# Two layers of cross-attention and routed experts on one core: from seven blocks with barriers to one block, with buffers placed by hand

## The chip, the cores and the metric

The kernel runs on one core of a Trainium2 chip. The metric is the device time of one execution in microseconds (us); lower is better. Five engines run their own instruction streams: PE (TensorE), DVE (VectorE), ACT (ScalarE), POOL (GpSimd) and SP (SyncE), which here only issues DMAs. They meet through semaphores.

## What is computed

4096 tokens (4 batches of 1024) with 256 features pass two layers in float32. Each layer adds a cross-attention over 64 context rows of its batch and then a feed-forward part with 8 experts:

```python
x = x + attention0(layernorm(x), ctx, mask)   # 8 heads of 64, masked keys
x = x + ffn0(layernorm(x))    # softmax router, best expert, capacity 640 rows, relu(x W1) W2, DFF 1024
x = x + attention1(layernorm(x), ctx)         # 16 heads of 64
x = x + ffn1(layernorm(x))    # best 2 of 8 experts, silu(x W11) * (x W12), then W2, DFF 512
```

A token over an expert's capacity in `ffn0` keeps its own row.

## The kernel before

The work is six stages, one after the other: setup of layer 0, attention of layer 0, experts of layer 0 (E0), setup of layer 1, attention of layer 1, experts of layer 1 (E1). A matrix product in float32 precision is made of three: every operand is split into a high part (`_hi`, written by ACT) and a rest (`_lo`, written by DVE or POOL), and hi·hi, hi·lo and lo·hi are summed in PSUM.

**Constants and setup** (`constants`, `attention_setup`, L130 to L359). DVE and POOL write constants in a first block (L159). Then SP loads the context, wk, wv, wqT, wo, the bias and the router, in layer 0 also x and the zero fills (L252 to L259, L189 to L199). PE makes keys and values, DVE puts them into `kd` and `vd` (L334 to L338), tiles that are cleared first (DVE L318, POOL L265). Then come the setup products: m = wqT·kd (PE L288; ACT `m_hi` L309; DVE `m_lo` L352), two psum tiles in turn in layer 1 and four in layer 0, and n = vd·wo with the bias (PE L297 to L300; ACT L314; DVE L357), over four psum banks. With m and n, attention needs only xn·m for the scores and prob·n for the output. All of m comes first, then all of n, b by b over the four batches.

**Attention** (`attention`, block at L487) runs over 32 tiles of 128 tokens in a software pipeline: iteration t goes from -8 to 36 and does, of different tiles, the gather of an expert's row (layer 1, t + 8, POOL L639), the statistics (t + 6), the normalisation `xn` (t + 5, L864), its transposes (t + 4, L527), the scores (t + 3, L546), maximum and exp (t + 2, ACT L604), the division (t + 1, POOL L636), the transposes of prob (t, L518), the output product (t, L561), the router (t - 3) and the scatter of rows to the experts (POOL L626). So the first useful exp comes at t = -2. Layer 1 ends with `plan` on DVE (L736 to L774), which makes the table `tab` of 39 tiles of 256 rows, with first row and expert of each. SP then writes 8 zero tails behind the experts' rows (L503 to L506).

**Experts.** `experts_capacity` (E0, block at L933) handles 8 experts of 640 rows: SP loads rows (L920), weights (L912, L916) and stores y (L956). Beside it, ACT and POOL split E1's raw weights (L1053, L1125), which SP loads and stores (L924, L929, L931). `experts_top2` (E1, block at L1189) loops over the 39 tiles: SP loads `E_up_w` (L1204), `w2` (L1212) and rows `xin` (L1219); PE transposes (L1239), multiplies up (L1266) and down (L1251); POOL adds the weighted rows into the output (L1386).

**What sets the order around the change.** Each stage is one or two blocks. At the end of a block every engine drains and meets a barrier. Between attention and experts `phase` (L120 to L128) also clears all semaphores and runs one more barrier. Buffers are opened and closed in stacks, so that the next stage's tiles may lie where the last one's were:

```python
def phase(self):
    self.nc.clear_and_free_semaphores(self.sems)
    self.sems = []
    self.nc.all_engine_barrier()
```

## Time and profile before

| | |
|---|---|
| median of 3 runs | 1207.63 us (1204.55 to 1209.05) |
| the profiled execution | 1209.9 us |
| its span in the profile | 1208.2 us |
| busy: PE / DVE / ACT / POOL | 1062.8 / 758.5 / 667.7 / 518.8 us |
| mean granted PE clock | 0.947 of full speed |
| moved by DMA | 159.36 MB, 181 GB/s over the span with both sides counted |
| chain that ended last | PE 21%, DMA 5%, DVE 2% of the span |

The span runs from the first to the last instruction; the execution's own time has 1.7 us around it. Timeline rows give start and duration in us, engine and line, operation with what it writes and reads, and in brackets how long the engine had been idle and what ended that. The stages lie in the span as follows: setup 0 until 37, attention 0 until 216, E0 from 220 to 468, setup 1 until 532, attention 1 with the plan until 820, E1 from 830 to the end.

### The profile page before, as it was taken

The page shows a single profiled execution, that of the slowest core. Times are in us where ns is not written, and L with a number is a line of the kernel's source. Part 1 is how long each engine was busy: PE and PEld are TensorE (multiplying, and loading weights), DVE is VectorE, ACT ScalarE, POOL GpSimd, SP SyncE. Part 2 cuts the span into 40 slices and gives each one's busy share as a digit, 9 for nine tenths or more (in the row PEclk, how much of TensorE's full clock was granted, in tenths as well). Part 3 has the DMA queues.
Part 4 walks back from the last instruction along what each step waited for, and adds up shares of the span by engine and source line. Part 5 has one row for each costly group of instructions (what it writes and reads, how often), then busy time and mean ns, then how long its engine had stood idle before and what let it go on. Part 6 is the DMA issues. An engine that isn't in the chain of part 4 may idle for free. (4 is left out here: it accounts for less than half of the span.)

```text
span 1208.2 us, 26203 instructions
## 1 busy us (share of the span) xinstructions
PE 1062.8 (88%) x7956; PEld 1000.7 (83%) x7956; DVE 758.5 (63%) x2287; ACT 667.7 (55%) x2466; POOL 518.8 (43%) x527
## 2 busy tenths in 40 slices
PE   6799995599999996868999999822999999999995
PEld 5588884599999995847999999822899999999995
DVE  6678876344444442675677777570776766766764
ACT  2588884344444440248999999711444444444442
POOL 1346776333333331035568887660233333333333
PEclk9899998699999997989999999965999999999998
DMA  8700001476666736001112221135557657388632
GB/s 298 310 2 23 28 32 47 167 249 219 218 218 217 235 110 182 4 23 31 36 47 75 76 72 63 54 133 211 150 141 218 164 144 232 57 280 253 162 62 35
DMA packets 86487, 159.36 MB, mean 132 GB/s; under 512 B 7682, under 2 KB 65924, under 8 KB 84356
## 3 DMA queue, kind: packets, MB, share of 16 engines
q1 hardware_dynamic: 69028, 131.20, 31.3%
q0 software_dynamic: 17376, 27.15, 10.9%
q8 instruction: 40, 0.66, 0.2%
q14 instruction: 43, 0.35, 0.1%
HBM read 157.37 MB, written 61.25 MB: 181 GB/s over the span
## 5 line engine op out<-in xcount | busy, mean ns | idle before, releaser
L1386 POOL DMA_INDIRECT out<-E_y,E_dest x78 | 121.1, 1553 | 262.1 <-DVE E_y L1347 241.8
L1266 PE MATMUL psum<-E_xT_hi,E_up_w 128*128 128x256 f32 x1248 | 225.1, 280 | 7.1 <-DMA E_up_w<-up 5.7
L604 ACT ACTIVATE L_prob<-psum,L_neg_max 128x64 f32<-128x64 f32 x768 | 228.6, 362 | 2.6 <-DVE L_neg_max L828 2.5
L1266 PEld LDWEIGHTS psum<-E_xT_hi,E_up_w 128*128 128x128 f32 x1248 | 194.1, 190 | 7.7 <-issue 6.0
L604 ACT ACTIVATION_READ_ACCUMULATOR L_prob<-psum,L_neg_max 128x1 f32 x768 | 195.3, 256 | 0.0
L1266 PE MATMUL psum<-E_xT_lo,E_up_w 128*128 128x256 f32 x624 | 174.3, 279 | 0.0
L1300 ACT ACTIVATE E_sg<-psum 128x256 f32<-128x256 f32 x156 | 60.0, 384 | 176.9 <-PE psum L1266 175.2
L1355 DVE TENSOR_TENSOR E_hf<-psum,E_sg 128x256 f32<-128x256 f32 x156 | 65.9, 422 | 94.8 <-ACT E_sg L1300 93.7
L561 PE MATMUL psum<-L_n_hi,L_pT_hi 128*128 128x256 f32 x384 | 109.6, 285 | 10.9 <-DVE L_pT_lo L835 10.9
L1266 PEld LDWEIGHTS psum<-E_xT_lo,E_up_w 128*128 128x128 f32 x624 | 118.4, 190 | 0.0
L636 POOL TENSOR_TENSOR L_prob<-L_prob,L_rcp 128x512 f32<-128x512 f32 (+1 forms) x64 | 94.3, 1474 | 37.4 <-DVE L_rcp L794 36.4
L561 PE MATMUL psum<-L_n_lo,L_pT_hi 128*128 128x256 f32 x384 | 109.3, 285 | 0.0
L561 PE MATMUL psum<-L_n_hi,L_pT_lo 128*128 128x256 f32 x384 | 109.3, 285 | 0.0
L1044 ACT ACTIVATE E_h_hi<-psum 128x256 fp32r<-128x256 f32 (+1 forms) x128 | 55.9, 437 | 89.3 <-PE psum L987 89.3
L1088 DVE SCALAR_TENSOR_TENSOR E_h_lo<-psum,E_h_hi 128x256 fp32r<-128x256 f32 (+1 forms) x128 | 62.8, 491 | 54.8 <-ACT E_h_hi L1044 54.1
L1004 PE MATMUL psum<-E_w_hi,E_h_hi 128*128 128x256 f32 x320 | 91.1, 285 | 0.0
L1004 PE MATMUL psum<-E_w_hi,E_h_lo 128*128 128x256 f32 x320 | 90.6, 283 | 0.0
L1004 PE MATMUL psum<-E_w_lo,E_h_hi 128*128 128x256 f32 x320 | 90.5, 283 | 0.0
L1251 PE MATMUL psum<-E_w_hi,E_h_hi 128*128 128x256 f32 x312 | 90.1, 289 | 0.0
L1251 PE MATMUL psum<-E_w_hi,E_h_lo 128*128 128x256 f32 x312 | 86.9, 279 | 0.0
L1251 PE MATMUL psum<-E_w_lo,E_h_hi 128*128 128x256 f32 x312 | 86.9, 279 | 0.0
L546 PE MATMUL psum<-L_m_hi,L_xT_hi 128*128 128x512 f32 x192 | 83.8, 437 | 3.4 <-ACT L_prob L604 3.4
(202 smaller groups left out, 3121.1 us busy)
## 6 DMA issues: line engine op xcount, KB each, us to landing
E_up_w<-up SPq DMA_DIRECT2D x39, 2048.0 KB
E_w<-in_w SPq DMA_DIRECT2D x39, 512.0 KB
w<-in_w SPq DMA_DIRECT2D x16, 1024.0 KB, 15.7
E_xin<-rows SPq DMA_DIRECT2D x39, 260.0 KB, 2.8
E_raw<-in_w SPq DMA_DIRECT2D x16, 512.0 KB, 6.9
up<-E_raw_hi SPq DMA_DIRECT2D x16, 512.0 KB, 5.9
up<-E_raw_lo SPq DMA_DIRECT2D x16, 512.0 KB, 3.7
rows<-zero SPq DMA_DIRECT2D x8, 640.0 KB
```

The costliest lines, as they stand in the source:

```text
L546: mm = e.matmul(bank, a[:, (t + 3) % 2, c, :], m[:, b, c, q * 512:(q + 1) * 512], start=(layer == 1 and c == 0 and j == 0), stop=(c == KC ...
L561: mm = e.matmul(o, a[:, r, :], m[:, b, r, :], start=(r == 0 and j == 0), stop=(r == PR - 1 and j == 2))
L604: last = e.activation(prob[:, q, h * KEYS:(h + 1) * KEYS], scores_ps(t)[:, h * KEYS:(h + 1) * KEYS], ACT.Exp, bias=nmx[:, q, h, :], accum_ ...
L636: e.tensor_tensor(pr, pr, rc[:, q, :, :].to_broadcast([P, H, KEYS]), ALU.mult).then_inc(s_p, 1)
L1004: mm = q.matmul(bank, a[:, h, m, c * P:(c + 1) * P], w[:, par, m, :], start=(k == 0), stop=(k == 3 * FC - 1))
L1044: q.activation(h_hi[:, h, m, 0:cn * P], ps[:, UP_BANK + m % 4, 0:cn * P], ACT.Relu).then_inc(s_hhi, 1)
L1088: q.scalar_tensor_tensor(h_lo[:, h, m, 0:cn * P], ps[:, UP_BANK + m % 4, 0:cn * P], 0.0, h_hi[:, h, m, 0:cn * P].bitcast(F32), ALU.max, AL ...
L1251: mm = q.matmul(ps[:, Y_BANK + c, 0:D], a[:, par, m, c * P:(c + 1) * P], w[:, par, m, :], start=(k == 0), stop=(k == 3 * FC - 1))
L1266: mm = q.matmul(bank, up_w[:, par, half, w, c, m * P:(m + 1) * P], x[:, c, :], start=(k == 0), stop=(k == 3 * KC - 1))
L1300: q.activation(sg[:, m, :], ps[:, UP_BANK + m, 0:T1], ACT.Silu).then_inc(s_sg, 1)
L1355: q.tensor_tensor(hf[:, m, :], ps[:, UP_BANK + m, T1:2 * T1], sg[:, m, :], ALU.mult).then_inc(s_hf, 1)
L1386: q.indirect_dma_start(p.out[:, :], bass.IndirectOffsetOnAxis(ap=dest[:, par, c, :], axis=0), y[:, par, c, :], None, compute_op=ALU.add).t ...
```

## The change

All stages now stand in one block, so each engine goes through all its stages without a barrier; counted waits on semaphores take the place of barriers. `phase`, the stacks and the clearing are gone. Semaphores with the same meaning serve both layers, and layer 1 waits for counts above those of layer 0 (`counted(base)`). Buffers have fixed places in one arena of 172 KiB (`p.at(kib, ...)`). Beyond that:

- The constants' block is gone; SP's first loads stand at the program's start. `kd` is cleared on POOL, ahead of `vd`. x is waited for by quarters.
- m of batch b is made in iteration t = b - 8 of the attention loop and n of batch b in t = b - 4, on PE, ACT and DVE. n has three psum banks (4 to 6) where it had four.
- SP loads w1 and w2 of expert 0 when n is done, E1's first raw weights when the last attention output is made, and expert 0's rows when the scatters have landed.
- The loads of setup 1 (ctxT, wk, wv, wqT) are issued inside E0's last expert. On ACT the last raw split stands inside that expert's hidden(7,1).
- The first four gathers of layer 1 have their own buffer. The 8 zero tails are issued by ACT, after its part of attention 1.
- For E1, SP waits for the table and the last scores, issues up(0) and w2(0), and only then waits for the scatters and issues xin(0).

The core of the diff:

```diff
-    def phase(self):
-        self.nc.clear_and_free_semaphores(self.sems)
...
-        self.nc.all_engine_barrier()
...
+    def at(self, kib, name, shape, dt=F32):
...
+        return self.nc.alloc_sbuf_tensor_at(name, shape, dt, offset=self.arena + int(kib * 1024))
...
+    N_BANK, RING_N = 4, 3
...
+    def loads(e):
...
+        else:
+            e.wait_ge(before.s_w1lo, E)
+            e.wait_ge(before.s_w2lo, E)
+            e.wait_ge(before.s_up, before.UPS * (E - 1))
+        e.dma_start(ctxT[:, :, :], ins["ctxT"].rearrange("(c p) k -> p c k", p=CP)).then_inc(s_w, 16)
...
+    def gpsimd(e):
+        if layer == 1:
+            e.wait_ge(before.s_rlo, 2 * E)
+            e.wait_ge(before.s_sthi, 16 * 2 * E)
+            e.wait_ge(before.s_stlo, 16 * 2 * E)
+        e.memset(kd[:, :, :, :], 0.0).then_inc(s_zero, 1)
+        if layer == 1:
+            e.wait_ge(before.s_up, before.UPS * E)
+        e.memset(vd[:, :, :, :], 0.0).then_inc(s_zero, 1)
...
+    def tensor_n(e, b):
...
+        for r in range(PR):
+            need(e, s_nlo, b * PR + r - RING_N + 1)
...
     def tensor(e):
+        e.wait_ge(p.s_sel, 3)
         for t in iters:
+            if ok(t + 8) and t < -4:
+                setup.tensor_m(e, t + 8)
+            if -4 <= t < 0:
+                setup.tensor_n(e, t + 4)
+            if t == -3:
+                setup.need(e, setup.s_mlo, setup.MS)
...
+            if t == 0:
+                setup.need(e, setup.s_nlo, setup.NS)
...
     def sync(q, late):
+        setup.need(q, setup.s_nlo, setup.NS)
+        load_w1(q, 0)
+        load_w2(q, 0)
+        rows_from.need(q, rows_from.s_out, NT)
+        for j in range(2):
+            load_raw(q, 0, j)
+        rows_from.rows_landed(q)
         load_x(q, 0)
-        for j in range(2):
-            load_raw(q, 0, j)
         load_w1(q, 1)
         load_w2(q, 1)
         for e in range(E):
             if e + 1 < E:
                 load_x(q, e + 1)
+            else:
+                late(q)
             store_raw(q, e, 0)
...
+                if m == 3 and (h == 0 or last):
+                    split_raw(e, h)
...
+        q.wait_ge(rows_from.s_tab, 2)
+        rows_from.need(q, rows_from.s_sim, NT)
+        load_up(0, 0)
+        load_w2(0, 0)
+        rows_from.rows_landed(q)
         load_x(0, 0)
-        load_up(0, 0)
-        load_w2(0, 0)
...
+        @block.scalar
+        def _(e):
+            att0.scalar(e)
+            exp0.scalar(e)
+            att1.scalar(e)
+            att1.tails(e)
+            exp1.scalar(e)
```

How the instructions move on SP at the end of E0. The kernel before, from the last expert's raw stores to the last load of setup 1; a branch is the end or the start of a block, where SP meets the other engines:

```order
L929 DMA up<-E_raw_hi 128x1024
L931 DMA up<-E_raw_lo 128x1024
L956 DMA rows<-E_y 128x3x256
L956 DMA rows<-E_y 128x2x256
L933 UNCONDITIONAL_BRANCH
L249 UNCONDITIONAL_BRANCH
L253 DMA L_ctxT<-in_ctxT 96x2x256
L254 DMA L_wk<-in_wk 96x2x1024
L255 DMA L_wv<-in_wv 96x2x1024
L256 DMA L_wqT<-in_wqT 128x8x256
L257 DMA L_wo<-in_wo 128x8x256
```

The changed kernel, the same stretch (the loads of the next setup are L266 to L269):

```order
L266 DMA L_ctxT<-in_ctxT 96x2x256
L267 DMA L_wk<-in_wk 96x2x1024
L268 DMA L_wv<-in_wv 96x2x1024
L269 DMA L_wqT<-in_wqT 128x8x256
L1021 DMA up<-E_raw_hi 128x1024
L1023 DMA up<-E_raw_lo 128x1024
L1021 DMA up<-E_raw_hi 128x1024
L1023 DMA up<-E_raw_lo 128x1024
L1053 DMA rows<-E_y 128x3x256
L1053 DMA rows<-E_y 128x2x256
L279 DMA L_wo<-in_wo 128x8x256
```

The four large loads of setup 1 have moved from behind two block ends to ahead of the last expert's raw stores; wo stays behind the last y store. No branch is left between the stages.

On ACT at the start of layer 1, before: the last two rows of n's loop, the blocks' seam and the first rows of attention:

```order
L314 ISA
L314 ACTIVATE L_n_hi<-psum 128x256
L310 REGISTER_ALU
L310 COMPARE_AND_BRANCH
L248 UNCONDITIONAL_BRANCH
L582 UNCONDITIONAL_BRANCH
L591 ACTIVATE L_xT_hi<-psum 128x256 x3
L604 ACTIVATE L_prob,L_sum<-psum,L_neg_max 128x64 x16
L591 ACTIVATE L_xT_hi<-psum 128x256
L604 ACTIVATE L_prob,L_sum<-psum,L_neg_max 128x64 x16
```

The changed kernel, from m to exp of tile 1 (L340 is n_hi, L657 xT_hi, L670 exp):

```order
L335 ACTIVATE L_m_hi<-psum 128x1024 x8
L340 ACTIVATE L_n_hi<-psum 128x256 x8
L657 ACTIVATE L_xT_hi<-psum 128x256
L340 ACTIVATE L_n_hi<-psum 128x256 x8
L657 ACTIVATE L_xT_hi<-psum 128x256
L340 ACTIVATE L_n_hi<-psum 128x256 x8
L657 ACTIVATE L_xT_hi<-psum 128x256
L670 ACTIVATE L_prob,L_sum<-psum,L_neg_max 128x64 x16
L340 ACTIVATE L_n_hi<-psum 128x256 x8
L657 ACTIVATE L_xT_hi<-psum 128x256
L670 ACTIVATE L_prob,L_sum<-psum,L_neg_max 128x64 x16
```

Before, all 32 copies of n end ahead of the first xT_hi. Now eight of them stand ahead of each of the first xT_hi, and the last eight behind exp of tile 0.

On SP between attention 1 and E1, before (rows<-L_zero is the last of the 8 tails; the TENSOR_LOAD reads a number of the table):

```order
L505 TENSOR_LOAD L_tail_i
L505 ISA x2
L506 ISA
L506 DMA rows<-L_zero 128x520
L487 UNCONDITIONAL_BRANCH
L1190 UNCONDITIONAL_BRANCH
L1215 TENSOR_LOAD tab
L1215 ISA x2
L1219 ISA
L1219 DMA E_xin<-rows 128x2x260
L1193 TENSOR_LOAD tab
```

The changed kernel, right behind SP's 32 stores of x:

```order
L1280 TENSOR_LOAD tab
L1280 ISA x2
L1291 ISA
L1291 DMA E_up_w<-up 128x4096
L1280 TENSOR_LOAD tab
L1280 ISA x2
L1299 ISA
L1299 DMA E_w_181<-in_w 128x4x256
L1302 TENSOR_LOAD tab
L1302 ISA x2
L1306 ISA
L1306 DMA E_xin<-rows 128x2x260
```

The tails are gone from SP (ACT has them), as are the block's ends; up and w2 of tile 0 now stand ahead of its rows.

## Rows read from the trace of the kernel before

**Rows 1.** Busy time, share and instructions of each engine, whole span

```profile
PE 1062.8 (88%) x7956; PEld 1000.7 (83%) x7956; DVE 758.5 (63%) x2287; ACT 667.7 (55%) x2466; POOL 518.8 (43%) x527
```

**Rows 2.** Busy by stretches: length, PE, PEld, DVE, ACT, POOL, PEclk, DMA, GB/s

```profile
497.00:560.00 63.00, 47.66 (x251) 37.30 (x250) 38.08 (x75) 32.92 (x111) 16.93 (x23) 0.89 0.06 17
...
800.00:846.00 46.00, 8.26 (x42) 7.74 (x43) 13.42 (x69) 4.02 (x7) 14.07 (x15) 0.50 0.56 207
...
846.00:1190.00 344.00, 335.35 (x2895) 333.48 (x2894) 243.31 (x730) 164.73 (x385) 114.91 (x74) 1.00 0.61 165
```

**Rows 3.** POOL's drains by line; ns min/median/max, first and last start

```profile
L487 POOLq DRAIN  x2: 2677/5295/7913, 216.6 to 820.7; - x2
...
L1189 POOLq DRAIN  x1: 3981/3981/3981, 1203.9 to 1203.9; - x1
```

**Rows 4.** SP's drain at L159; timeline of layer 0's start, SP, PE, ACT

```profile
L159 SPq DRAIN  x1: 7/7/7, 0.8 to 0.8; - x1
...
3.03 0.40 SPq L252 DMA_DIRECT2D L_keep_u<-in_mask  x1
...
8.76 5.71 PE L277 MATMUL psum<-L_ctxT,L_wk 96*128 96x256 f32 x16 [8.76 <-DMA L_wk<-in_wk]
...
19.01 7.41 PE L288 MATMUL psum<-L_kd,L_wqT 128*128 128x128 f32 x64 [1.08 <-DVE L_vd L334]
...
34.27 1.56 PE L297 MATMUL psum<-L_wo,L_vd 128*128 128x256 f32 x6
...
49.63 0.31 ACT L604 ACTIVATE L_prob<-psum,L_neg_max 128x64 f32<-128x64 f32 x1 [0.55 <-DVE L_neg_max L828]
```

**Rows 5.** Timeline between attention 0 and E0, SP and PE

```profile
220.45 0.37 SPq L920 DMA_DIRECT2D E_xin<-rows  x1
...
224.97 2.40 PE L967 MATMUL psum<-ident,E_xin 128*128 128x128 f32 x10 [17.07 <-DMA E_xin<-rows]
```

**Rows 6.** Timeline, E0's end to m of layer 1, SP, PE, DVE, POOL

```profile
454.79 0.33 SPq L931 DMA_DIRECT2D up<-E_raw_lo  x1
...
468.99 0.35 SPq L253 DMA_DIRECT2D L_ctxT<-in_ctxT  x1
...
465.04 0.28 PE L1004 MATMUL psum<-E_w_lo,E_h_hi 128*128 128x256 f32 x1
...
476.81 10.65 PE L277 MATMUL psum<-L_ctxT,L_wk 96*128 96x256 f32 x32 [11.49 <-DMA L_wk<-in_wk]
...
495.62 3.84 PE L288 MATMUL psum<-L_kd,L_wqT 128*128 128x128 f32 x32 [1.26 <-DVE L_vd L334]
...
488.48 7.08 DVE L334 COPY L_vd<-psum 64x256 f32<-64x256 f32 x16
...
469.30 3.51 POOL L265 MEMSET L_vd<- 128x4096 f32 x1 [14.54 <-POOLq L127]
```

**Rows 7.** Timeline of layer 1's setup products and first exps, PE and ACT

```profile
512.57 0.60 PE L297 MATMUL psum<-L_wo,L_vd 128*128 128x256 f32 x2
...
526.92 3.48 PE L297 MATMUL psum<-L_wo,L_vd 128*128 128x256 f32 x14
...
547.35 0.31 ACT L604 ACTIVATE L_prob<-psum,L_neg_max 128x64 f32<-128x64 f32 x1 [0.66 <-DVE L_neg_max L828]
...
553.58 0.31 ACT L604 ACTIVATE L_prob<-psum,L_neg_max 128x64 f32<-128x64 f32 x1 [1.12 <-DVE L_neg_max L828]
```

**Rows 8.** Timeline between attention 1 and E1, DVE, SP and PE

```profile
813.57 0.25 DVE L770 TENSOR_TENSOR tab<-L_ra 128x37 int32<-128x37 f32 x1
...
807.38 9.30 SPq L506 DMA_DIRECT2D rows<-L_zero  x8
...
831.67 0.37 SPq L1204 DMA_DIRECT2D E_up_w<-up  x1
...
833.13 1.12 PE L1239 MATMUL psum<-ident,E_xin 128*128 128x128 f32 x4 [29.15 <-DMA E_xin<-rows]
...
839.90 0.55 PE L1266 MATMUL psum<-E_xT_hi,E_up_w 128*128 128x256 f32 x1 [5.66 <-DMA E_up_w<-up]
```

More of the change, by code:

```diff
@@ L105, in more, with counted, need @@
             n -= 1
+class Stage:
+    pass
+def counted(base):
+    def need(eng, sem, value):
+        if not is_int(value) or value > 0:
+            eng.wait_ge(sem, base.get(sem, 0) + value)
+    return need
 class Program:
@@ L203, with attention_setup @@
 ZEROED = 16 * (2 * E + 2)
-def attention_setup(p, layer, ins, st):
-    nc = p.nc
+VECTOR = 2 * E + 1
+def attention_setup(p, layer, ins, base, before):
     H = 8 if layer == 0 else 16
@@ L374, in attention @@
+    return st
+def attention(p, layer, ins, setup, base, before):
+    ps = p.psum
+    m_hi, m_lo, n_hi, n_lo, masked, wr = setup.m_hi, setup.m_lo, setup.n_hi, setup.n_lo, setup.masked, p.wr[layer]
     H = 8 if layer == 0 else 16
@@ new lines, in attention @@
+    xfT = at(94 if layer == 0 else 154, "xfT", [P, KC, P])
+    if layer == 1:
+        place["next"] = 163
+    nmx, sm, rc = (small(x, [P, 2, H, 1]) for x in ("neg_max", "sum", "rcp"))
+    stats = small("stats", [P, 2, 2, 6])
+    mv = small("mv", [P, 4, 2, 2])
+    ve = small("var_eps", [P, 4, 2])
+    rs = small("rstd", [P, 4, 2])
+    nb2 = small("nb2", [P, 4])
+    if layer == 1:
+        assert place["next"] <= 164
+        place["next"] = 155
+    lg = small("lg", [P, 2 * G, E])
+    sh, sh2, ex, a1, a2, pos = (small(x, [P, G, E]) for x in ("sh", "sh2", "ex", "a1", "a2", "pos"))
@@ L872, in experts_capacity, with sync, tails @@
-def experts_capacity(p, ins):
-    nc, ps = p.nc, p.psum
+    def sync(e):
+        if layer == 1:
+            out_t = p.out[0:TOK, :].rearrange("(t p) d -> p t d", p=P)
+            for t in range(NT):
+                need(e, s_res, t + 1)
+                e.dma_start(out_t[:, t, :], p.x[:, t, 0:D]).then_inc(s_store[t % 4], 16)
+    def tails(e):
+        need(e, s_zero, 1)
+        need(e, s_tab, 1)
+        for j in range(E):
+            r = e.value_load(tail_i[0:1, j:j + 1], min_val=0, max_val=IDLE_ROW - T1)
+            e.dma_start(p.d1[bass.ds(r, T1), :].rearrange("(p c) d -> p (c d)", p=P), zero[:, :]).then_inc(s_tail, 16)
@@ new lines, in gpsimd, with add, body @@
+    def gpsimd(q):
+        def add(i, par):
+            wait(q, s_add, 16 * TC * i)
+            for c in range(TC):
+                wait(q, s_y, TC * i + c + 1)
+                land(q, i)
+                q.indirect_dma_start(p.out[:, :], bass.IndirectOffsetOnAxis(ap=dest[:, par, c, :], axis=0),
+                                     y[:, par, c, :], None, compute_op=ALU.add).then_inc(s_add, 16)
+        def body(i, par, last):
+            if not is_int(i) or i > 0:
+                add(i - 1, 1 - par)
+            if last:
+                add(i, par)
+        rows_from.x_stored(q)
+        tiles_loop(q, body)
+        q.wait_ge(s_add, 16 * TC * NT1)
```

2158 lines of the change are left out of this document (1099 added, 1059 removed).

## The prediction

> **What bounds the kernel now.** I read the engines' busy times first, then the busy time by stretches, then the barriers, then the timeline around each seam. TensorE is busy 1062.8 of 1208.2 us [rows 1]; ACT has 55% and nothing else comes near it. Inside the loops there is little to find: from 846 to 1190 PE is busy 335.35 of 344 us [rows 2]. The 145 us in which PE rests lie mostly where stages meet: 15.3 us of 497 to 560, 37.7 of 800 to 846 [rows 2], 17.07 before the first expert [rows 5] and 11.49 after the last [rows 6]. What ends those waits is not arithmetic. At each seam every engine stops at a block's end, GpSimd drains (2.68 and 7.91 us, both with all its scatters landed [rows 3]), a barrier follows, and only then does SP issue the loads of the next stage. So the bound of this change is the chain at six places, each priced below. The loops' instructions and their order are the same before and after, so I price them at nothing; what covers that is only that buffers at other addresses run alike, a rival below.
>
> **1. The start.** SP stood ready at 0.8 us but issued its first load at 3.03, after a barrier; the first product waits for wk until 8.76 [rows 4]. The new kernel has no barrier there: 3.03 - 0.8 = 2.2 us. The kd memset goes from DVE to POOL (2048 columns; 4096 take 3.51 us in layer 1 [rows 6], so 1.8 us) and ends before data can land. Bounds 0 and -2.2; taken **-2.2**.
>
> **2. Layer 0's ramp.** Before, m runs from 19.01 to 26.42, n until 34.27 + 1.56 = 35.8, a barrier follows, then the pipeline fills until exp of tile 1 begins at 49.63 [rows 4]: 30.6 us from m's start. The change puts m into iterations -8 to -5 and n into -4 to -1, so filling and n run together. From there on: m 7.4, four n of (35.8 - 26.4) / 4 = 2.35 each are 9.4, exp of tile 0 on ACT ahead of n(3) is half of layer 1's 6.2 (8 heads for 16), so 3.1, and some 1.2 us of normalising, transposing and maxima put between in each of four iterations, 4.8: 24.7 in all, where 30.6 was. Bounds: 0 if nothing overlaps, and -11 if all of n and the barrier vanish. The n ring has 3 banks for 4, so I give back 0.2: **-5.7**.
>
> **3. Layer 0 to expert 0.** GpSimd has seen the last scatter land at 216.6 [rows 3], SP issues xin at 220.45, PE starts at 224.97 [rows 5]. Now SP itself waits for the scatters and issues at once, some 0.3 later: 216.9 - 220.45 = -3.6. The two raw loads (1 MB) were issued behind xin and are now ahead, during the scatters, so xin may also land up to 1 us sooner. w1 and w2 of expert 0 are loaded as before, hidden by 160 us of attention. Bounds -3.3 and -4.7; taken **-3.6**.
>
> **4. End of the experts to m of layer 1.** PE ends at 465.32, SP issues ctxT at 468.99, kv products wait for wk until 476.81 and then again for DVE; m starts at 495.62 [rows 6]. The change issues ctxT, wk, wv, wqT (2.7 MB) on SP inside expert 7, about 438, behind its wait for the last w1 and w2 splits and ahead of the raw stores of that expert. Then only DVE's 32 copies remain: 7.08 / 16 = 0.44 each [rows 6], 14.1 us, with 1 us around: m at 465.3 + 15.1 = 480.4, **-15.2**. The cover is thin in one place: POOL clears kd only after the raw stores landed (the last was issued at 454.79; I allow 2.7 us), then vd, 2 x 3.51 us: 464.5, against 465.3 [rows 6]. Every microsecond by which the stores are late behind the new loads counts in full beyond the first. So bounds -11 and -15.5. What is late next at this seam is DVE.
>
> **5. Layer 1's ramp.** From m's start to exp of tile 1: 553.58 - 495.62 = 58.0 us, in which n takes (526.92 + 3.48 - 512.57) / 4 = 4.46 per batch of eight [rows 6, 7]. Now: m 512.57 - 495.62 = 17.0; n with three banks, each waiting for the copy three back instead of four, 4.46 x 1.15 = 5.1, so n(0) to n(2) 15.3; exp of tile 0, in order on ACT ahead of n(3), 553.58 - 547.35 = 6.2; n(3) 5.1; and some 6 us of other work in between: 49.6. **-8.4**. The first gathers, which stood behind the barrier before, go out under m. Bounds: 0 if all is serial, and -17 if all four n are hidden. Between so far ends I stand in the middle, since ACT and DVE carry both halves. The trace grants 0.89 of the clock in this stretch [rows 2], most of it at 2.4 GHz. The Trainium skill, *TensorE: Matmul & The Clock Gate*, Part 1, speaks against spreading work so: an array that rests often falls to 1.2 GHz. By that rule n would wait for PE as well and the term would be nearer -5 than -8.4; the rows before, where n held the full clock while paced by ACT, speak for the larger one.
>
> **6. Layer 1 to the last stage.** The plan's table is ready at 813.57 + 0.25, the scatters have landed by 820.7 [rows 3, 8], but xin goes out only after the barrier and up behind it at 831.67, transposes start at 833.13, and the first product waits for up until 839.90 [rows 8]. Now SP sends up(0) and w2(0) first, as soon as the table stands: read the expert, issue at 814.8, land 8.1 later at 823. xin goes at 821.4, lands behind 2.5 MB at about 825.2, against 833.13 before, and from transposes to first product I allow 2.6 (transposes 1.1, ACT 0.6, DVE 0.7): 827.8. **-12.1**; bounds -9 and -14. The eight zero stores took SP until 816.68 [rows 8]; on ACT they no longer stand ahead of the up load. Two of them are still to come at 814.8. The Trainium skill, *DMA: Bandwidth & Descriptors*, § Issuing engines are not separate DMA queues, says that a second issuing engine saves only the issuing, as all transfers share the same 16 engines. By that rule up lands up to 1.5 us later and the term is -11; no row before shows stores and this load together.
>
> **Sum:** -2.2 - 5.7 - 3.6 - 15.2 - 8.4 - 12.1 = -47.2. The profiled execution took 1209.9 us; the median of the runs is 1207.63, 2.3 lower. 1209.9 - 47.2 = 1162.7, and against the median 1160.4. I forecast **1161 us**.
>
> **The rivals.** *The drain is saved up.* Before, GpSimd's drain took 2.68 us after 32 indirect transfers, 7.91 after 96, 3.98 after 78 [rows 3]: it grows with the transfers, though all had landed. If one drain at the end settles all 206, it brings back 10.6 us: 1171. For it: 0.084 and 0.082 us per transfer, the same twice. Against it: 0.051 in the last stage, which does not fit a plain sum. *The ramps stay serial.* n and the filling both need ACT and DVE in order; if terms 2 and 5 are nothing, 1160.4 + 14.1 = 1175. Against it: PE, ACT and DVE all rest in 497 to 560 [rows 2]. *The early loads collide.* 2.7 MB ahead of expert 7's stores hold up ACT's split_raw(7,1), now in the middle of hidden(7,1), and so PE's psum ring, and the memsets of term 4: up to 5 us, 1166. *Slower than before.* The last stage has PE at 97% [rows 2]. If the hand-placed tiles make its loads or reads slower, every one of 39 tiles pays; it must be 47 + 6 = 53 us, or 1.4 us on each tile of 344 / 39 = 8.8 us, before the kernel is slower by 0.5%: 1215 at 1.4. Against it: same shapes, same engines, same order. *It does not do what it says.* An engine still waits at the seams, since counted waits replace barriers one for one: some 1200. The order of instructions shows the moves on every engine, so little for it.
>
> **How the numbers follow.** Forecast 0.62; drain saved up 0.15; ramps serial 0.1; collision 0.09; unchanged 0.02; slower 0.02. The forecast's own range is 1152 to 1168: the bounds of terms 3, 4 and 6 together give 8, the ramps a few more. To keep four in five with the drain and the serial ramps inside, I go to 1150 and 1177. Under 1202 is faster by 0.5%, about what a measurement of this kernel can tell from no change: 0.96; within 0.5% 0.02; slower 0.02.
>
> **What would show it.** Right, if the changed profile has kv's first product within 1 us of the last expert product, m of layer 1 some 15 us after it, n products of layer 1 between transposes of xn, PE's wait ahead of the last stage near 24 us instead of 36, and loops of the old length (attention 1 about 8 us a tile, last stage 8.8). Wrong in term 5, if exp of tile 1 comes more than 53 us after m's start; wrong in term 4, if DVE waits for the memsets. A last drain above 10 us means the first rival. If the stretch of 39 tiles is longer than 350 us, the fourth.

## The result, and the profile after

The changed kernel takes **1186.85 us** (median of 4 runs, 1184.48 to 1190.26) where the kernel before takes 1206.66 beside it: ratio 0.984, 95% interval 0.980 to 0.987. It is faster, by 19.8 us. The forecast was 1161 with a range of 1150 to 1177: the sign is right, the size is not. The profiled execution took 1190.3 us, its span is 1188.5 (before 1209.9 and 1208.2).

The engines' busy times come first, since one line there already speaks against the forecast. The same 7956 products keep PE busy for 1072.5 us, 9.7 more than before [rows 1], though the PE clock was granted at 0.958 instead of 0.947:

```profile
PE 1072.5 (90%) x7956; PEld 1011.1 (85%) x7956; DVE 754.2 (63%) x2285; ACT 667.1 (56%) x2466; POOL 526.2 (44%) x529
```

Then the timeline at the seams, in order of time, PE, ACT and DVE (start and duration in us, engine, line, operation, idle time before it and what ended it):

```profile
6.64 5.55 PE L301 MATMUL psum<-L_ctxT,L_wk 96*128 96x256 f32 x16 [6.64 <-DMA L_wk<-in_wk]
16.73 7.41 PE L312 MATMUL psum<-L_kd,L_wqT 128*128 128x128 f32 x64 [1.08 <-DVE L_vd L357]
26.23 0.67 PE L326 MATMUL psum<-L_wo,L_vd 128*128 128x256 f32 x2 [2.09 <-issue]
...
44.88 0.31 ACT L670 ACTIVATE L_prob<-psum,L_neg_max 128x64 f32<-128x64 f32 x1 [0.89 <-DVE L_neg_max L903]
...
219.25 2.37 PE L1060 MATMUL psum<-ident,E_xin 128*128 128x128 f32 x10 [14.58 <-DMA E_xin<-rows]
...
459.36 7.07 PE L301 MATMUL psum<-L_ctxT,L_wk 96*128 96x256 f32 x32
...
474.98 3.84 PE L312 MATMUL psum<-L_kd,L_wqT 128*128 128x128 f32 x32 [1.64 <-DVE L_vd L357]
...
528.79 0.32 ACT L670 ACTIVATE L_prob<-psum,L_neg_max 128x64 f32<-128x64 f32 x1 [1.45 <-DVE L_neg_max L903]
...
787.32 0.25 DVE L840 TENSOR_TENSOR tab<-L_ra 128x37 int32<-128x37 f32 x1
...
804.13 1.08 PE L1328 MATMUL psum<-ident,E_xin 128*128 128x128 f32 x4 [26.40 <-DMA E_xin<-rows]
...
806.69 0.58 PE L1355 MATMUL psum<-E_xT_hi,E_up_w 128*128 128x256 f32 x1 [1.48 <-DVE E_xT_lo L1415]
```

Most rows have their partner of before in [rows 4] to [rows 8], and the differences divide the whole span without a remainder:

| stretch | before | after | change | forecast |
|---|---|---|---|---|
| start to m | 19.01 | 16.73 | -2.3 | -2.2 |
| m to exp of tile 1, layer 0 | 30.62 | 28.15 | -2.5 | -5.7 |
| attention 0, to its last scatter | 163.95 | 167.10 | +3.1 | 0 |
| last scatter to E0's transposes | 11.39 | 7.27 | -4.1 | -3.6 |
| E0, to its last product | 240.07 | 239.99 | -0.1 | 0 |
| last product to m of layer 1 | 30.58 | 15.74 | -14.8 | -15.2 |
| m to exp of tile 1, layer 1 | 57.96 | 53.81 | -4.2 | -8.4 |
| attention 1, to the table | 259.99 | 258.53 | -1.5 | 0 |
| table to E1's first product | 26.33 | 19.37 | -7.0 | -12.1 |
| E1, first to last up product | 348.9 | 361.5 | **+12.6** | 0 |
| from there to the end | 19.4 | 20.3 | +0.9 | 0 |

Stretches are taken from start to start, so attention 0 ends where its last scatter starts. Three seams came as forecast (-2.3, -4.1, -14.8). Two ramps (the stretches in which a layer's pipeline fills) and the last seam gave 13.7 where 26.2 was expected, and the last stage, whose instructions and order are the same, lost 12.6. The parts are read from one execution of each kernel. The windows of E1, before:

```profile
839.90:1188.80 348.90, 340.25 (x2911) 338.38 (x2912) 242.78 (x727) 165.97 (x386) 114.91 (x74) 0.99 0.62 169
```

and after (length, PE, PEld, DVE, ACT, POOL, PEclk, DMA share, GB/s):

```profile
806.70:1168.20 361.50, 353.48 (x2912) 351.63 (x2913) 243.86 (x727) 166.36 (x387) 114.93 (x74) 0.99 0.60 161
```

PE is busy for 13.2 us more over the same number of products, at the same mean clock; DVE, ACT and POOL do the same work in the same time. So it is no wait: the products themselves are slower. Where an up stream runs undisturbed, the timeline shows by how much. Before (a pair with xT_hi and one with xT_lo make three products):

```profile
960.19 0.28 PE L1266 MATMUL psum<-E_xT_lo,E_up_w 128*128 128x256 f32 x1
960.31 0.40 PE L1266 MATMUL psum<-E_xT_hi,E_up_w 128*128 128x256 f32 x2
...
962.66 0.28 PE L1266 MATMUL psum<-E_xT_lo,E_up_w 128*128 128x256 f32 x1
```

After:

```profile
959.99 0.28 PE L1355 MATMUL psum<-E_xT_lo,E_up_w 128*128 128x256 f32 x1
960.11 0.40 PE L1355 MATMUL psum<-E_xT_hi,E_up_w 128*128 128x256 f32 x2
...
961.07 0.28 PE L1355 MATMUL psum<-E_xT_lo,E_up_w 128*128 128x256 f32 x1
```

Before, 21 products start in 962.66 - 960.19 = 2.47 us, one every 118 ns; after, 9 in 1.08, one every 120. Over all of E1 before, the distance of these up products is 113 or 114 ns in some tiles and 117 to 119 in the others, mean 115.4; after it is 120 for 1756 of 1805. For products of 256 columns in attention and E0 the median is 120 in both kernels. With 72 such products in a tile (48 up, 24 down), 39 tiles and some 4.4 ns, that is about 12 us.

What could set it? The SBUF addresses differ in one thing. In E1 before, xin is 4160 bytes long, so that up_w and w2 lie 448 bytes above a multiple of 512 and xT and h, which follow xin, lie on one. A product has two operands in SBUF, the tile that PE loads as weights (here xT or h) and the tile that it streams (here up_w or w2): in E1 before they start 64 bytes apart, modulo 512. In the split products of all other stages, and everywhere in the new arena, they are equal modulo 512. The absolute place alone can't be it: n and pT of attention 1 before lie on multiples of 512 as xT and h do, and have 120. That is the **placement** theory; its rivals are that the missing barriers, the absolute addresses or the loop's code slow PE.

### The profile page after: what moved, and what is told of

It is laid out like the page before. It is cut to its first block, busy times and chain, and to the rows that moved or that the text cites. A ratio compares the mean times of both kernels' runs of the same rounds, so it can differ in the third digit from the quotient of the medians.

```text
span 1188.5 us, 25824 instructions
## 1 busy us (share of the span) xinstructions
PE 1072.5 (90%) x7956; PEld 1011.1 (85%) x7956; DVE 754.2 (63%) x2285; ACT 667.1 (56%) x2466; POOL 526.2 (44%) x529
## 4 chain that ended last, share of the span: by engine, by line
PE 74%; DMA 8%; DVE 8%; ACT 4%; issue 3%; POOL 3%; SPq 0%; DVEq 0%; ACTq 0%; POOLq 0%
PE psum L1355 13%; PE psum L624 11%; PE psum L609 10%; PE psum L1079 9%; PE psum L1096 8%; PE psum L1340 7%; DMA E_xin<-rows 5%; PE psum L581 3%; PE psum L326 2%; PE psum L630 2%; ACT L_prob L670 2%; PE psum L312 1%; PE psum L1328 1%; POOL rows L691 1%; PE psum L596 1%
## 5 line engine op out<-in xcount | busy, mean ns | idle before, releaser
L1355 PE MATMUL psum<-E_xT_hi,E_up_w 128*128 128x256 f32 x1248 | 233.7, 285 | 2.9 <-DVE E_xT_lo L1415 2.9
L670 ACT ACTIVATE L_prob<-psum,L_neg_max 128x64 f32<-128x64 f32 x768 | 229.2, 363 | 4.8 <-DVE L_neg_max L903 4.7
L1355 PEld LDWEIGHTS psum<-E_xT_hi,E_up_w 128*128 128x128 f32 x1248 | 199.6, 194 | 3.5 <-DVE E_xT_lo L1415 3.5
L670 ACT ACTIVATION_READ_ACCUMULATOR L_prob<-psum,L_neg_max 128x1 f32 x768 | 195.7, 257 | 0.0
L1355 PE MATMUL psum<-E_xT_lo,E_up_w 128*128 128x256 f32 x624 | 177.8, 285 | 0.0
L1355 PEld LDWEIGHTS psum<-E_xT_lo,E_up_w 128*128 128x128 f32 x624 | 121.0, 194 | 0.0
L624 PEld LDWEIGHTS psum<-L_n_hi,L_pT_hi 128*128 128x128 f32 x384 | 73.6, 192 | 14.7 <-issue 12.3
## 6 DMA issues: line engine op xcount, KB each, us to landing
rows<-zero SPq DMA_DIRECT2D x8, 640.0 KB, 14.8
```

What stands on the lines that cost most here:

```text
L624: mm = e.matmul(o, a[:, r, :], m[:, b, r, :], start=(r == 0 and j == 0), stop=(r == PR - 1 and j == 2))
L670: last = e.activation(prob[:, q, h * KEYS:(h + 1) * KEYS], scores_ps(t)[:, h * KEYS:(h + 1) * KEYS], ACT.Exp, bias=nmx[:, q, h, :], accum_ ...
L1355: mm = q.matmul(bank, up_w[:, par, half, w, c, m * P:(m + 1) * P], x[:, c, :], start=(k == 0), stop=(k == 3 * KC - 1))
```

## The experiments

Each set ran on one chip, with the kernel before beside it. The unaltered changed kernel ran twice more: 0.985 (0.982 to 0.988) and 0.984 (0.981 to 0.986) of the kernel before, medians 1193.5 and 1192.8 us.

### Placement in E1

```diff
-    xT_hi, xT_lo = ... ((56, "xT_hi"), (58, "xT_lo")))
+    xT_hi, xT_lo = ... ((56 + 64 / 1024, "xT_hi"), (58 + 64 / 1024, "xT_lo")))
-    h_hi, h_lo = ... ((95, "h_hi"), (103, "h_lo")))
+    h_hi, h_lo = ... ((95 + 64 / 1024, "h_hi"), (103 + 64 / 1024, "h_lo")))
```

> The changed kernel, but in the last stage (E1) xT_hi, xT_lo, h_hi and h_lo lie 64 bytes further up in SBUF (y and the small tiles after them move up too), so that the tiles PE loads as weights and the tiles it streams (up_w, w2_hi, w2_lo) differ by 64 bytes modulo 512, as they did in the kernel before; in the changed kernel they are equal modulo 512. Placement theory: the 256-column products of E1 come every 113 to 118 ns again instead of every 120, the stretch of 39 tiles falls from 361 to about 350 us, and the time by 10 to 13 us, to about 1175. Rival (the missing barriers, or the absolute place of the streamed tiles, or the loop's code, make E1 slower): pitch stays at 120 and the time within 2 us of the changed kernel's.

Measured: 1189.8 us, 0.980 (0.976 to 0.983) of the kernel before. The unaltered changed kernel did not run on this chip; against its 0.984 and 0.985 on others the intervals overlap, so the time alone doesn't show the gain, and the expected 1175 was not reached. The trace shows it: mean distance of the products 116.6 ns, and PE's busy time in E1 9.3 us lower than in the changed kernel's first profile (7 to 8 lower than in its two later ones):

```profile
816.50:1171.10 354.60, 344.14 (x2912) 342.28 (x2913) 243.39 (x727) 166.40 (x387) 114.94 (x74) 0.99 0.61 162
```

The other way round, the kernel before with a pad and nothing else:

```diff
         xin = p.sb(st, n + "xin", [P, 2, TC, DW])
+        pad = p.sb(st, n + "pad", [P, 112])
         xT_hi, xT_lo = ...
```

> The kernel before, with an unused tile of 448 bytes between xin and xT_hi in E1, so that xT and h are equal to up_w and w2 modulo 512, as in the changed kernel. Nothing else is touched. Placement theory: the E1 products slow from a pitch of 113 to 118 ns to 120, and the time grows by 10 to 13 us to about 1218. Rivals (barriers, code): no change within 2 us.

Measured: 1219.9 against 1212.0 us, 1.007 (1.004 to 1.009). The kernel before, with all its barriers, now has the distance of 120 ns (1799 of 1806 up products), and PE is busy 11.6 us longer:

```profile
838.00:1192.90 354.90, 351.89 (x2911) 350.09 (x2912) 244.00 (x727) 165.81 (x386) 114.91 (x74) 0.99 0.62 167
```

So barriers, code and absolute place are out: 64 bytes of relative placement switch it on and off in both kernels. Both effects on the time came below the 10 to 13 us expected, for a reason that the traces show. E1 grew by 6.0 us here, though PE was busy for 11.6 more, because it waited less for rows: 1.6 us in all for E_xin, where it is 7.2 in the kernel before. Those waits lie where the expert changes and rows come late behind new weights; a faster PE runs into them. In the first profile of the changed kernel they stayed (6.5 us), so there nearly all of the slower products counted: PE was busy for 13.2 us more, of which some 1.7 come from 3.4 us at half the clock at 983, and the waits took 0.6 less. In its two later profiles E1 took 358.4 and 356.4 us. So the placement is worth roughly 6 to 12 us of E1, by how many of the waits take it up.

Two kernels with other offsets, one execution each (1186.0 and 1192.7 us), for the distances alone:

> The changed kernel, with E1's xT 32 bytes and h 128 bytes further up: two more offsets, one for the up products (xT against up_w) and one for the down products (h against w2). Placement theory: any offset that is not a multiple of 512 gives a pitch below 120 ns in its own products; if the size of the offset matters, the up products at 32 and the down products at 128 show different pitches. Rival: 120 in both.

> The changed kernel, with E1's xT 256 bytes and h 96 bytes further up. As in the run before it: placement theory says below 120 ns in at least one of the two; a pitch of 120 for the offset of 256 alone would say that what counts is the offset modulo 256 or less. Rival: 120 in both.

Mean distance in ns: offset 32 in the up products 116.8, 64 in both 116.6 and 116.7, 96 in the down products 118.5, 128 there 119.0, 256 in the up products 119.8, none 120.0 (up) and 119.5 (down). Small offsets help, an offset of 256 hardly does: that part of the expectation ("any offset") fell, and what counts may be the offset modulo 256 rather than 512, which no run here separates. PE's own rate depends on how its two SBUF operands lie to each other. The Trainium skill, *SBUF — State Buffer*, § SBUF: two separate sides, says that on the engines' side only a port pair shared by two other engines causes contention and that PE never waits on anyone. That is about one engine holding up another; it says nothing of PE's own two operands, where these runs find the difference. What inside the chip does it, no run here shows.

### The ramps

All of m and n ahead of the pipeline again, without the barrier:

```diff
-            if ok(t + 8) and t < -4:
-                setup.tensor_m(e, t + 8)
-            if -4 <= t < 0:
-                setup.tensor_n(e, t + 4)
+            if t == -8:
+                for b in range(B):
+                    setup.tensor_m(e, b)
+                for b in range(B):
+                    setup.tensor_n(e, b)
```

(likewise on ACT and DVE; the first gathers use the tile of the later ones.)

> The changed kernel, but all of m and then all of n are made in the first iteration of attention in both layers, ahead of the pipeline's filling, as before, only without the barrier; the first gathers wait for m. Theory (n and the filling run in order on ACT and DVE, so running them together gives little): from the first product of m to exp of tile 1 some 29.5 us in layer 0 (28.2 in the changed kernel) and 57 in layer 1 (53.9), 4 to 5 us in all, the time about 1191. The forecast's terms 2 and 5 say 5.7 and 8.4, so 13 to 14 us. Rival (the interleave gives nothing, all of it was the barrier): within 1 us of the changed kernel.

Measured: 1209.7 us, 0.998 (0.995 to 1.000). That is 16 us slower than the changed kernel beside it (1193.5), where I had expected 1191. Layer 0, then layer 1:

```profile
18.20 7.41 PE L312 MATMUL psum<-L_kd,L_wqT 128*128 128x128 f32 x64 [1.05 <-DVE L_vd L357]
27.71 0.67 PE L326 MATMUL psum<-L_wo,L_vd 128*128 128x256 f32 x2 [2.10 <-issue]
...
51.54 0.32 ACT L672 ACTIVATE L_prob<-psum,L_neg_max 128x64 f32<-128x64 f32 x1 [0.55 <-DVE L_neg_max L906]
...
480.49 5.47 PE L312 MATMUL psum<-L_kd,L_wqT 128*128 128x128 f32 x32 [1.48 <-DVE L_vd L357]
...
543.21 0.31 ACT L672 ACTIVATE L_prob<-psum,L_neg_max 128x64 f32<-128x64 f32 x1 [1.12 <-DVE L_neg_max L906]
```

From m to exp of tile 1: 33.3 and 62.7 us, against 28.1 and 53.8 in the changed kernel. My theory of the small interleave fell: the interleave is worth 5.2 + 8.9 = 14.1 us, the sum of terms 2 and 5. That the two agree to the tenth is chance, for the clock has a part in the measured one. From m to exp of tile 1 in layer 1, the changed kernel in its first profile and the serial run (length, PE, PEld, DVE, ACT, POOL, PEclk, DMA share, GB/s):

```profile
474.98:528.79 53.81, 45.17 (x242) 35.77 (x243) 33.28 (x69) 26.11 (x76) 9.63 (x15) 0.94 0.04 11
480.49:543.21 62.72, 49.46 (x236) 37.48 (x237) 34.30 (x69) 26.77 (x77) 12.66 (x18) 0.86 0.05 15
```

PE was granted 0.86 of its clock in the serial ramp and was busy 4.3 us longer, so up to that much of the 8.9 may be the clock's; the kernel before had 0.90.

Serial in the new kernel is also slower than serial was before (30.6 and 58.0, barrier included). So the change adds something to both ramps. From n's first to its last product it takes 10.4 and 21.3 us here, 9.2 and 17.4 before; the ring of three banks for n is the likely reason, but no run changes it alone, and in layer 1 a part of n ran at half the clock here (501.2 to 508.0) and none before. The other piece is the rest between m and n, 2.1 us before n at 27.71. DVE splits the bias only behind the last m_lo, where before it did so ahead of m:

```diff
-        if b == B - 1:
+        if b == 1:
             vector_bias(e)
```

> The changed kernel, but DVE splits the bias of wo after batch 1 of m instead of after batch 3. In the changed kernel PE rests between m and n: n starts 2.3 us after m's last product in layer 0 and 3.3 in layer 1, where before it was 0.2 and 0.1. Theory: these waits are DVE's, which makes bo_hi and bo_lo behind the last m_lo, and they are the larger part of what terms 2 and 5 missed; now n starts within 1.5 us of m's end, and exp of tile 1 comes 1 to 2 us sooner in layer 0 and 2 to 3 in layer 1: 3 to 5 us in all. Rival (PE waits for something else there, or DVE is the bound of the whole ramp anyway, so that the work is only moved): n starts sooner, but exp of tile 1 comes at the same distance from m, within 1 us.

Measured: 0.982 (0.980 to 0.985), beside 0.984 for the unaltered kernel, 1.6 us that the intervals do not separate. The trace does:

```profile
24.59 0.60 PE L326 MATMUL psum<-L_wo,L_vd 128*128 128x256 f32 x2
...
42.86 0.32 ACT L670 ACTIVATE L_prob<-psum,L_neg_max 128x64 f32<-128x64 f32 x1 [0.88 <-DVE L_neg_max L903]
...
526.52 0.31 ACT L670 ACTIVATE L_prob<-psum,L_neg_max 128x64 f32<-128x64 f32 x1 [1.46 <-DVE L_neg_max L903]
```

PE's rest before n is gone (m began at 17.34 and 474.88) and the ramps are 25.5 and 51.6 us, where the unaltered kernel beside it has 28.1 and 53.5. A part may again be the clock: the unaltered kernel had 3.4 us at half of it in layer 0's ramp and 6.8 in layer 1's, this one none and 3.4. That the profile called the rest "issue", not a wait for DVE, was misleading.

### The seam after E0

```diff
             if e + 1 < E:
                 load_x(q, e + 1)
-            else:
-                late(q)
...
+        late(q)
```

> The changed kernel, but ctxT, wk, wv and wqT of layer 1 are loaded behind the last y store of E0, as before, only without the barrier. Term 4 theory: the early loads are worth what PE waited for wk, 11.5 us, less the 3 to 4 that the barrier cost: kv starts 6 to 9 us after the last product of E0 and m of layer 1 comes 21 to 25 us after it where it is 14.7 now; 7 to 10 us slower. Rival (kv would start as early, as DVE or the memsets bound it): within 2 us. The stores of the last raw splits then land sooner, so ACT's wait of 4.1 us ahead of raw_hi of (7,1) goes, at no gain in the time.

Measured: 1207.2 us, 0.996 (0.995 to 0.998); the profiled execution is the fastest of its runs, 1200.9.

```profile
469.42 10.32 PE L301 MATMUL psum<-L_ctxT,L_wk 96*128 96x256 f32 x32 [8.89 <-DMA L_wk<-in_wk]
...
487.90 2.27 PE L312 MATMUL psum<-L_kd,L_wqT 128*128 128x128 f32 x18 [1.26 <-DVE L_vd L357]
```

m of layer 1 comes 27.7 us after E0's last product (15.8 with the early loads on this chip, 30.6 before). So of term 4 the early loads bring 12 us and the barrier 3. I had expected 7 to 10 for the loads. A part that I had left out is that the first kv products take 10.32 us instead of 7.07: behind PE's rest of 8.89 us they run at half the clock until 475.8.

### The opening of E1

```diff
-        load_up(0, 0)
-        load_w2(0, 0)
         rows_from.rows_landed(q)
         load_x(0, 0)
+        load_up(0, 0)
+        load_w2(0, 0)
```

> The changed kernel, but SP waits for the scatters and issues xin(0) before up(0) and w2(0), the order of before without its barrier. In the changed kernel xin was issued 9.2 us after the last scatter had ended on POOL, where 2.9 would do. Theory that the 2.5 MB of up and w2 slow the last scatters and tails and hold xin back: xin goes out some 6 us sooner, lands 2.5 us later, but up is then issued 6 us later than before and takes 8.2: first product 1 to 3 us sooner than in the changed kernel. Rival (the forecast's reasoning: up first is right, the scatters are late for another reason): xin is issued at the same time and up comes 8 us behind it, first product 5 to 6 us later.

> The changed kernel once more, unaltered, on the chip of the three runs beside it, so that they have a partner there. Both theories: 0.98 to 0.987 of the kernel before, pitch 120 ns in E1. Open is whether DVE's plan takes 7.5 us on this chip, as in the first profiles, or 17.5, as in the four runs of the first set; with 17.5 the table, not the scatters, would set the start of E1, and the changed kernel loses up to 10 us there.

On this chip the plan on DVE took 17.9 us instead of 7.4, so in both runs the table came last. Unaltered (two of DVE's small steps, SP, PE):

```profile
787.63 0.16 DVE L817 TENSOR_TENSOR L_tiles<-L_tiles,L_base 128x1 f32<-128x1 f32 x1 [0.54 <-issue]
789.03 0.16 DVE L817 TENSOR_TENSOR L_tiles<-L_tiles,L_base 128x1 f32<-128x1 f32 x1 [1.24 <-issue]
...
801.57 0.36 SPq L1291 DMA_DIRECT2D E_up_w<-up  x1
...
804.30 0.38 SPq L1306 DMA_DIRECT2D E_xin<-rows  x1
...
812.01 1.09 PE L1328 MATMUL psum<-ident,E_xin 128*128 128x128 f32 x4 [32.97 <-DMA E_xin<-rows]
```

Rows first:

```profile
802.43 0.41 SPq L1306 DMA_DIRECT2D E_xin<-rows  x1
803.63 0.37 SPq L1291 DMA_DIRECT2D E_up_w<-up  x1
...
805.27 1.09 PE L1328 MATMUL psum<-ident,E_xin 128*128 128x128 f32 x4 [26.15 <-DMA E_xin<-rows]
812.28 0.55 PE L1355 MATMUL psum<-E_xT_hi,E_up_w 128*128 128x256 f32 x1 [5.92 <-DMA E_up_w<-up]
```

Behind up and w2 the rows need 7.7 us from issue to PE, alone 2.8. From the table, the first product comes 1.7 us sooner with the rows first (12.7 for 14.4; 2.3 sooner in the span, as the table stood 0.6 earlier); in the time (0.985 for both) it does not show. This left open why xin went out so late in the first profile of the changed kernel, where the table stood early. There SP waited 9.3 us for the scatters; the waits of SP from 788 to 802 (total, times, longest):

```profile
SPq L99 <- DMA rows<-x,L_row: 9.3, 1, 9.3
```

Two runs settle it: up(0) and w2(0) long before the scatters end, or right beside them.

```diff
-        q.wait_ge(rows_from.s_tab, 2)
         rows_from.need(q, rows_from.s_sim, NT)
-        load_up(0, 0)
-        load_w2(0, 0)
+        q.dma_start(up_w[:, 0, ...], up_d[0, :, :]).then_inc(s_w[0], 16)
+        q.dma_start(w2[:, 0, :, :], w2_d[:, 0, :, :]).then_inc(s_w2[0], 16)
         rows_from.rows_landed(q)
+        q.wait_ge(rows_from.s_tab, 2)
         load_x(0, 0)
```

> The changed kernel, but SP issues up(0) and w2(0) as soon as the last scores are made, some 35 us before the table stands, for expert 0 (whose rows tile 0 holds as long as expert 0 has any, as it has in these inputs); then it waits for the scatters, then for the table, then issues xin. Theory (what holds xin back in the changed kernel is the 2.5 MB in flight, ahead of xin or beside the last scatters): scatters landed 2.9 us after POOL's last one ended, xin landed 2.9 us after its issue, and first product 5 to 8 us sooner against the end of the table or of the tails than in the two runs of the unaltered kernel, where it came 14.4 us after the table; the time 4 to 8 us below the changed kernel. Rival (xin is late for another reason): xin still takes 7 to 8 us, same time.

> As the run before it, but up(0) and w2(0) are held back until the scatters of the last tile but two have landed, so that their 2.5 MB are in flight together with the last four scatters, as in the first profile of the changed kernel, whatever the table does. Theory of the shared queues: SP sees the last scatters landed 6 to 9 us after POOL's last one ended, instead of 2.9. Rival: 2.9 as without the load, and the wait of 8 us in the first profile came from elsewhere.

Long before (1184.5 us, 0.979, 0.975 to 0.983; POOL's last scatter, SP, PE):

```profile
770.17 0.45 SPq L1309 DMA_DIRECT2D E_up_w<-up  x1
...
794.18 0.96 POOL L691 DMA_INDIRECT rows<-x,L_row  x1 [0.30 <-issue]
...
798.03 0.41 SPq L1306 DMA_DIRECT2D E_xin<-rows  x1
...
801.09 1.08 PE L1329 MATMUL psum<-ident,E_xin 128*128 128x128 f32 x4 [20.30 <-DMA E_xin<-rows]
```

Beside them (1189.1 us, 0.980, 0.975 to 0.985):

```profile
793.37 0.34 SPq L1313 DMA_DIRECT2D E_up_w<-up  x1
...
794.57 0.96 POOL L694 DMA_INDIRECT rows<-x,L_row  x1 [0.30 <-issue]
...
805.17 0.41 SPq L1309 DMA_DIRECT2D E_xin<-rows  x1
...
807.98 1.09 PE L1333 MATMUL psum<-ident,E_xin 128*128 128x128 f32 x4 [26.53 <-DMA E_xin<-rows]
```

POOL ends its last scatter at the same time in both, but SP sees the scatters landed 1.5 us after that in the first (796.6) and 8.2 us after it in the second (803.7): the loads hold back the word that the scatters have landed until they are nearly through themselves. PE's first product of E1 comes 13.3 us after the table in the first and 19.2 in the second. The times of the two (0.979 and 0.980) don't separate them, nor either clearly from the 0.984 of the unaltered kernel, which did not run on this chip; that the gain is there rests on the traces. The Trainium skill, *DMA: Bandwidth & Descriptors*, § Queues, rings and completion order, says that a semaphore's increment lands only after every earlier write of the same DMA engine, in whatever queue. These two runs agree with it: in the second the last increment of the scatters comes at 803.75, between up's own last one (803.3) and that of w2 (804.9), 10 us after the two were issued.

### All stages

```diff
-    xT_hi, xT_lo = ... ((70, "xT_hi"), (72, "xT_lo")))
+    xT_hi, xT_lo = ... ((70.0625, "xT_hi"), (72.0625, "xT_lo")))
-    pT_hi, pT_lo = ... zip((78, 80) if layer == 0 else (146, 150), ...
+    pT_hi, pT_lo = ... zip((78.0625, 80.0625) if layer == 0 else (146.125, 150.125), ...
...
-    h_hi, h_lo = ... ((16, "h_hi"), (40, "h_lo")))
+    h_hi, h_lo = ... ((16.5, "h_hi"), (40.5, "h_lo")))
```

(and the tiles beside them moved to make room, E0's w1_hi to w2_lo by 64 bytes, E1 as above)

> The changed kernel, unaltered, as the partner of the three beside it: 0.98 to 0.987 of the kernel before.

> The changed kernel with the tiles that PE loads as weights and those it streams 64 bytes apart modulo 512 in all stages: xT and pT against m and n in both attentions, w1 and h against xT and w2 in E0, and E1 as in the run with 64 bytes. Placement theory, if it holds for every stage: the pitch of 256-column products falls from 120 to 113 to 118 ns in E0 and the attentions too, a tile of attention 1 from 7.38 to about 7.25 us where PE is the bound, 15 to 25 us in all, about 1170 to 1178. Rival (it holds only for E1's loads, which run while 2 MB weights are loaded, or a stage is paced by DVE or ACT): only E1's 6 us.

Measured: 1184.6 us, 0.977 (0.975 to 0.979), against 0.984 unaltered. The distances of 256-column products fall to 113 to 118 ns in every stage. Attention 1, unaltered, then with offsets, a stretch in which PE never rests:

```profile
540.00:740.00 200.00, 200.00 (x1459) 186.53 (x1458) 149.99 (x457) 185.12 (x977) 146.66 (x170) 1.00 0.18 60
```

```profile
540.00:740.00 200.00, 200.00 (x1476) 184.58 (x1475) 149.56 (x461) 186.60 (x983) 147.79 (x171) 1.00 0.18 60
```

1.2% more products in the same time; a tile takes 7.30 us instead of 7.38, and an expert of E0 29.1 instead of 29.6. The whole is 8.3 us, about half of the least that was expected, and from E1 no more came than in its own run. The forms of the products say a part of why. Median distances, unaltered and with offsets, in ns: 256 columns in attention 1 120 and 113, in E0 120 and 117; but 512 columns (the scores) 231 and 234, 384 columns (E0's up products) 173 and 174. Of these only the 256-column form gains, the longer ones lose a little, and the scores are 12 x 231 of a tile's 7380 ns. The other part may be the clock: granted was 0.952 to 0.957 in the six executions with offsets and 0.957 to 0.960 in the five without, and the profiled ones have 116.0 and 102.5 us at half of it. E0 as a whole took 240.8 us in both, though each of its middle experts was 0.5 us faster. Attention 0 hardly moved (4.68 against 4.70 us a tile).

With the bias early and the rows first:

> The last one with the bias split early and with the rows ahead of up and w2 at the start of E1 (2.3 us sooner to the first product in its own run). If the three add up: 5 to 7 us below the run with offsets in all stages, and the fastest of all. If the early bias only moves work, 2 us below it.

Measured: 1181.9 us, 0.975 (0.972 to 0.978), 2.6 us below the run before it where 5 to 7 were expected, and by the intervals not separated from it. And with up and w2 right behind the last scores in the place of the rows first:

> The fastest kernel so far (offsets in all stages, bias early) with the loads of up(0) and w2(0) right behind the last scores, as in the first of these three. Theory: a further 5 to 7 us below it, 0.968 to 0.971 of the kernel before, about 1175. Rival: as fast as it, 0.975.

Measured: **1166.6 us** against 1210.1, 0.964 (0.960 to 0.968), the fastest kernel of this study and further down than the 0.968 to 0.971 expected. The runs on the same chip had 0.979 with the opening alone; the 0.975 comes from another chip, and a part of the step from there is the chip's: the plan took 17.7 us there and the table came 5.8 us after POOL's last scatter, here it took 7.6 and came before. It serves inputs in which expert 0 gets a row. PE is busy for 1050.9 us in it, 21.6 less than in the changed kernel's first profile. Its opening of E1, xin 2.9 us after POOL's last scatter has ended:

```profile
779.87 0.96 POOL L691 DMA_INDIRECT rows<-x,L_row  x1 [0.30 <-issue]
...
783.72 0.41 SPq L1306 DMA_DIRECT2D E_xin<-rows  x1
...
789.02 0.58 PE L1356 MATMUL psum<-E_xT_hi,E_up_w 128*128 128x256 f32 x1 [1.48 <-DVE E_xT_lo L1416]
```

## Why the prediction was right or wrong

Of the 47.2 us forecast, 19.7 came in the span. Of the missing 27.5, terms 2, 5 and 6 account for 12.6 and the loops, priced at nothing, for 15.1; the other three terms brought 0.2 more than forecast.

**Terms 1, 3 and 4 held** (-2.3, -4.1, -14.8 against -2.2, -3.6, -15.2). The thin cover of term 4 held too: ACT's last raw split waited for a store, but kd was clear at 457.2 and vd at 460.7, and DVE had to wait 0.6 us for it, the sign set for a wrong term 4, which here cost too little to move it. What is late next there is DVE's 32 copies, as forecast.

**"The loops ... I price them at nothing"** is the step that failed most: +12.6 in E1 and +3.1 in attention 0. The first is the sentence "what covers that is only that buffers at other addresses run alike". The fourth rival named the place and the test (a stretch of 39 tiles over 350 us; it was 361.5), but priced it by loads or reads at 1.4 us a tile and gave it 0.02; it was 0.3 us a tile, in PE's own operands, and small enough to leave the sign alone. [Rows 2] had 2895 products in 335.35 us; taking the distance of 256-column products stage by stage from that trace (115 ns in E1, 120 elsewhere) would have shown that E1 ran faster and that there was something to lose.

The 3.1 of attention 0 are two pieces. One is a scatter of 2.59 us where others take 0.96, 1.6 more:

```profile
207.29 2.29 DVE L1163 TENSOR_TENSOR E_w_lo<-E_w,E_w_hi 128x2048 fp32r<-128x2048 f32 x1
207.82 2.59 POOL L691 DMA_INDIRECT rows<-L_stage,row  x1 [0.30 <-issue]
```

This one is the change's own. Without the barrier DVE begins with expert 0's weights (`E_w_lo`) while POOL still scatters; before, the same instruction came at 222.42, behind the seam. All fifteen traces of changed kernels have the slow scatter beside it, the two of the kernel before (one with the pad) have neither. Why POOL slows there, no run shows. The other piece is 3.4 us at half the clock near 184: it stands in eight of the fifteen traces, and attention 0 takes about 1.5 us less in the seven without it.

**Term 2 and term 5** (-2.5 for -5.7, -4.2 for -8.4). The gain of running n and the filling together is of the forecast size, 14.1 us, up to 4.3 of it the clock's. Missing is the wait of n for the bias, 2.1 and 3.1 us: it stands in the code that was moved (the bias is split behind the last m_lo, on DVE, in order) and I went from m straight to n in both sums. With the bias early, layer 0 takes 25.5 where 24.7 was worked out, layer 1 51.6 where 49.6 was. The factor 1.15 that term 5 took for three banks had no row behind it, nor had the 0.2 us of term 2; the serial run has 21.3 us of n for 17.4 (1.22, the clock included) and in layer 0 10.4 for 9.2. The clock, which I had weighed against this term, did not cost it: granted in this ramp was 0.94, and 0.90 before. The sign set for a wrong term 5, more than 53 us, came (53.8).

**Term 6** (-7.0 for -12.1). I had xin issued at once when the scatters are out, and only its own landing lengthened by up and w2. The loads stand ahead of the scatters' completion too: in the first profile the scatters' last increment came 8.0 us after POOL's last one had ended (800.1 against 792.1), before 1.7 (820.0 against 818.3). Up itself landed 10.1 us after its issue where 8.1 was worked out, and PE didn't wait for it. From POOL's last scatter to the first product it is 21.6 us before, 14.6 in the changed kernel and 8.5 with the loads issued long before: loading up first saved PE's wait for up, but about 6 us more were to be had. On chips where the plan is slow the table comes last instead and hides this.

**The rivals.** The drain was not saved up: POOL's only drain takes 4.89 us, 0.9 more than before, for 206 transfers [rows 3]:

```profile
L1505 POOLq DRAIN  x1: 4889/4889/4889, 1183.4 to 1183.4; - x1
```

The ramps did not stay serial, as the serial run shows. The early loads collided with the raw stores, ACT waited 4.1 us, and PE lost nothing.

## What to carry to other kernels

When buffers move, compare the start-to-start distance of equal products between stages and kernels: the same instruction at the same clock may run 2 to 6% apart. Here, 32 to 64 bytes between PE's weights and its streamed tile, modulo 512 (by the run with 256 bytes perhaps modulo 256), brought most of it back for 256-column products; those of 384 and 512 columns lost about 1% (1 and 3 ns). Do not issue a large load shortly before small transfers whose landing somebody waits for: issue it long before, or behind. When a loop's parts are moved between queues, follow also the small helpers at their ends (here two bias instructions) to who waits for them.
